# The last stage of a graph network on one core: eight units in the ring of gathered rows in place of six

## The reference, cut to what matters

```python
h = (xn @ W).reshape(N, HEADS, HEAD_DIM)          # 8 heads of 32
a_src = jnp.einsum('nhd,hd->nh', h, att_src)
a_dst = jnp.einsum('nhd,hd->nh', h, att_dst)
e = jax.nn.leaky_relu(a_src[src] + a_dst[dst], NEG_SLOPE)
ee = jnp.exp(e - emax[dst])
alpha = ee / denom[dst]
agg = jax.ops.segment_sum(h[src] * alpha[:, :, None], dst, num_segments=N)
out = layer_norm(agg.reshape(N, 256) + xn @ W_res + bias, ln2_g, ln2_b)
x = x + out + gelu_tanh(out @ ffn_w1 + ffn_b1) @ ffn_w2 + ffn_b2
# then, on the normed x: eight experts of three 256x256 layers each (batch norm, relu),
# summed with softmax weights, and added to x
```

## Time and profile before

| | us |
|---|---|
| median of the timed runs | 2847.34 |
| span of the profiled execution | 3261.7 |
| the last stage in it, from its first gather to its end | 1461.2 to 3261.7 |
| TensorE matmul busy, whole span | 2445.7 (75%) |
| VectorE busy | 1927.4 (59%) |
| GpSimd busy | 1783.5 (55%) |
| ScalarE busy | 1330.1 (41%) |
| gathers of the last stage (line 2766), 784 | 905.8 busy |

### The profile page before, as it was taken

One profiled execution on the slowest core, in us unless ns is written; L12 is line 12 of the kernel. 1 busy time (PEld: TensorE's weight loads), 2 busy tenths in 40 slices (PEclk: granted clock), 3 DMA queues, 4 the chain that ended last, 5 costly groups with the idle time before them and its releaser, 6 DMA issues.

```text
span 3261.7 us, 50094 instructions
## 1 busy us (share of the span) xinstructions
PE 2445.7 (75%) x16869; PEld 1988.4 (61%) x16869; DVE 1927.4 (59%) x5122; ACT 1330.1 (41%) x2771; POOL 1783.5 (55%) x1695
## 2 busy tenths in 40 slices
PE   8437677567676768661567888899888898898998
PEld 8325455345554547660356766777677676686887
DVE  8733344344344447764466676677776676686754
ACT  6303233222222324440234454555544555464665
POOL 6366666666666660837665574465744556464000
PEclk9667777778877778785688998999998999898999
DMA  9443334334443331276467675576765767576534
GB/s 324 142 129 113 118 117 122 110 109 118 119 121 118 113 100 28 88 227 184 138 208 235 191 233 158 181 233 206 224 204 161 219 198 219 177 219 193 160 119 140
DMA packets 312865, 531.11 MB, mean 163 GB/s; under 512 B 89679, under 2 KB 210322, under 8 KB 312598
## 3 DMA queue, kind: packets, MB, share of 16 engines
q1 hardware_dynamic: 234021, 312.19, 30.5%
q0 software_dynamic: 75264, 212.04, 22.8%
q10 hardware_dynamic: 3312, 3.55, 0.4%
HBM read 454.05 MB, written 73.54 MB: 162 GB/s over the span
## 4 chain that ended last, share of the span: by engine, by line
PE 30%; another core or an unknown queue 9%; DVE 6%; issue 5%; ACT 2%; POOL 1%; DMA 1%; SPq 1%; DVEq 0%; POOLq 0%; ACTq 0%
PE PB L125 25%; PE PB L2793 2%; POOL G L2766 1%; DVE G L3092 1%; ACT TFm L3006 1%; DVE XR L3273 1%; DVE H2l L3261 1%; PE PB L2804 0%; DVE H1l L3261 0%; DMA G<-tab,SRCL 0%; PE PB L2845 0%; DVE HT9l L3182 0%; PE PB L2814 0%; PE PB L2880 0%
## 5 line engine op out<-in xcount | busy, mean ns | idle before, releaser
L2766 POOL DMA_INDIRECT G<-tab,SRCL x784 | 905.8, 1155 | 694.8 <-PE PB L2793 442.8
L1194 POOL DMA_INDIRECT GE<-tab,SRCL x748 | 724.0, 968 | 393.9 <-issue 204.1
L3006 ACT ACTIVATE TFm<-PB,BIA,SCL 128x512 f32<-128x512 f32 (+2 forms) x416 | 312.8, 754 | 474.4 <-PE PB L125 226.0
L125 PE MATMUL PB<-YTMh,MW 128*128 128x512 f32 (+2 forms) x832 | 303.8, 416 | 51.6 <-ACT TFm L3006 36.4
L125 PE MATMUL PB<-H1h,MW 128*128 128x512 f32 (+2 forms) x832 | 299.8, 412 | 37.9 <-issue 29.0
L125 PE MATMUL PB<-MW,H2h 128*128 128x256 f32 x1568 | 301.4, 291 | 27.3 <-issue 20.3
L125 PEld LDWEIGHTS PB<-MW,H2h 128*128 128x128 f32 x1568 | 253.9, 197 | 36.1 <-issue 24.9
L3092 DVE TENSOR_TENSOR G<-G 128x1024 f32<-128x1024 f32 x196 | 238.1, 1216 | 2.7 <-DVE G L3086 2.2
L125 PE MATMUL PB<-MW,H2l 128*128 128x256 f32 x784 | 224.7, 287 | 4.7 <-issue 4.7
L1578 ACT ACTIVATE TF<-PB,fb 128x256 f32<-128x256 f32 (+1 forms) x200 | 93.6, 472 | 323.1 <-remote 165.9
L125 PEld LDWEIGHTS PB<-YTMh,MW 128*128 128x128 f32 x832 | 167.7, 204 | 93.9 <-issue 42.8
(11 more groups left out here) (365 smaller groups left out, 6614.6 us busy)
## 6 DMA issues: line engine op xcount, KB each, us to landing
MW<-msplit SPq DMA_DIRECT2D x312, 512.0 KB
ROW<-relrow SPq DMA_DIRECT2D x196, 96.0 KB
msplit<-FWs SPq DMA_DIRECT2D x68, 256.0 KB
part<-ZERO SPq DMA_DIRECT2D x2, 6600.0 KB
G<-tab,SRCL POOLq DMA_INDIRECT x784
GE<-tab,SRCL POOLq DMA_INDIRECT x748
part<-WIN SPq DMA_DIRECT2D x262, 33.0 KB
SUMa<-part SPq DMA_DIRECT2D x49, 132.0 KB
```

The lines of the kernel that those rows point to most:

```text
L125: ins = pe.matmul(ps, lhs(p), rhs(q), start=(first and i == 0), stop=(last and i == 2), skip_group_check=True)
L1194: po.indirect_dma_start(c.GE[:, (s - 2 * UE) % RU, q, 0:256], None, c.tab0, bass.IndirectOffsetOnAxis(ap=c.SRCL[:, 2 * s + q:2 * s + q + 1 ...
L2766: po.indirect_dma_start(b.G[:, j % RP, u, :], None, c.tab1, bass.IndirectOffsetOnAxis(ap=c.SRCL[:, 4 * j + u:4 * j + u + 1].bitcast(U32), ...
L3006: a.activation(b.TM[:, m, 0:n], PB[of][:, 0:n], ACT.Relu, bias=b.BIA[:, l, q:q + 1], scale=b.SCL[:, l, q:q + 1]).then_inc(S.h2_relu if l e ...
```

## The change

The ring of gathered rows gets two more places, and its semaphores two more names. `RP` stands in the allocation of `G8` (`[P, RP, 4, 272]`, 4,352 bytes per partition and place), in GpSimd's wait and place, in VectorE's and TensorE's place, in the count that VectorE waits for (`64 * (j // RP + 1)`) and in the scheduler's rule above.

```diff
-RP = 6
+RP = 8
@@ def g_in(S, r):
-    return (S.g_in0, S.g_in1, S.g_in2, S.g_in3, S.g_in4, S.g_in5)[r]
+    return (S.g_in0, S.g_in1, S.g_in2, S.g_in3, S.g_in4, S.g_in5, S.g_in6, S.g_in7)[r]
@@ def last_layers(nc, c, A, out):
-    S = named(nc, c, "last", "dve consts g_in0 g_in1 g_in2 g_in3 g_in4 g_in5 nd_in0 ...
+    S = named(nc, c, "last", "dve consts g_in0 g_in1 g_in2 g_in3 g_in4 g_in5 g_in6 g_in7 nd_in0 ...
```

More of the change, by code:

```diff
@@ L3291, in last_layers @@
 def last_layers(nc, c, A, out):
-    S = named(nc, c, "last", "dve consts g_in0 g_in1 g_in2 g_in3 g_in4 g_in5 nd_in0 nd_in1 nd_in2 nd_in3 row_in0 row_in1 rowhot onehot "
+    S = named(nc, c, "last", "dve consts g_in0 g_in1 g_in2 g_in3 g_in4 g_in5 g_in6 g_in7 nd_in0 nd_in1 nd_in2 nd_in3 row_in0 row_in1 rowhot onehot "
                              "nd_mm factor product edge_mm evac placed sum_in0 sum_in1 sums self_in0 self_in1 self_in2 self_in3 "
```

## The result

The changed kernel takes 2823.2 us (median of 4 runs, 2819.75 to 2827.59) against 2848.71 us for the kernel before (4 runs, 2845.98 to 2856.44). The ratio is 0.9903, 95% interval 0.9885 to 0.992: 25 to 28 us faster, where 7 us were forecast and 2828 us was the lower end of the range.

What follows compares the result with a forecast made beforehand. TensorE was taken to carry the last stage, with 227 us idle in its middle part. Removing one late-gather event gave 7 us, order counted 0: 2847.3 - 7 = 2840.3 us; 8-in-10 range 2828 to 2859 us.

Steps and rivals of the forecast that it cites:

- the ring runs tight more often than here: Timed runs: if gather instructions don't shrink with the rest, 980 us of gathers stand in a shorter last stage.
- The mechanism: Units 109 to 111: GpSimd's ring wait makes gathers late, VectorE waits at line 3083, TensorE stops 4.45 and 0.99 us.
- The number of places: Last stage from 1580 us: one late-gather event on the chain, units 109 to 111; units 57, 72 and 168 outside it.
- one event of 7.5 us on the chain: Units 109 to 111: VectorE's waits of 0.18, 1.13 and 6.23 us all go; 7 us taken as the gain.
- Rival 3: Ring tight in every 48-unit repeat of the timed runs: 13 to 18 us off, about 2832 us; chance 0.14.
- The limit by VectorE: At units 109 to 111, VectorE without its 6.23 us wait is busy without a break, so at most 7.5 us gained.
- The order: Planner reads RP, so later due times may reorder every engine's list; counted 0, range -11 to +11 us.
- Rival 4: Later due times make VectorE delay weigh and sums; TensorE idle grows 5%: +11 us, 2858 us; chance 0.25.
- The start-up and the last unit: Start-up doesn't count, ring not yet full; unit 195 loses its 34.44 us gather wait but gains nothing in the same order.
- What would show it: Changed trace: line 2793 wait some 400 us, gather waits under 2 us after 1600 us, no late-gather TensorE stop over 4 us.
- The 76.1 us under the name of the first layer's gather: Line 3083 waits from 1580 us on, attributed to some other transfer; 76.1 us should stay after the change.
- earlier gathers would slow others: Gathers brought forward share 16 DMA engines with the weights; part of the "nothing" rival, 2847 us, chance 0.25.

Runs made afterwards that it cites:

- eight with the small memset: Changed kernel plus a 128x128 GpSimd memset ahead of each unit: ratio to the kernel before 0.9991 at 3250 us speed; 2827.45 us, 0.9923 at the other.

## Why the prediction was wrong, point by point

**The trace was that of another speed.** This is the step that failed. The prediction said that the timed runs were not this trace, that the gather instruction would not shrink with the rest, and that "the ring runs tight more often than here", and then took the forecast from the trace all the same. At 2856 us the last stage took 2854.4 - 1307.0 = 1547 us against 1801 us in the earlier trace rows, and GpSimd's gathers needed 1000.07 us of it against 905.85 us. The prediction's own figure for that case, 196 x 5.0 = 980 us, was too small as well: a unit took 1229.9 / 196 = 6.3 us. GpSimd's share of the stage went from 50% to 65%, and in its middle from 55% to 73% (741.93 of 1014 us).

**The mechanism was right.** A ring wait, then gathers that come too late, VectorE at line 3083, a split queued behind it, TensorE stopped and its clock down: the walk through the earlier trace rows holds step for step at units 72 to 74. The price of a place was right in kind too: the longest of the three waits there is followed by two stops of TensorE, 2.38 and 1.05 us, and a clock of 0.56.

**The number of places was mis-sized.** This is the term of the sum that the wrong trace spoiled. The sum had one event of 7.5 us on the chain and 3.2 us of waits outside it, 10.7 us in all behind the start-up. At the right speed line 3083 waited 33 us for gathers behind unit 65, in five places. Rival 3 had this, with the repeat every 48 units and unit 72 and 168 as its evidence, and gave 2832 us with a chance of 0.14; its own price, three or four times 4.45 us, was too small as well. It left out what the forecast counted: the lower clock behind each stop, 12.3 us of TensorE's busy time. Whether 7 us would be right at the 3250 us speed is not shown: that would be a ratio of 0.998, and the interval of seven places there, 0.9971 to 1.0084, takes in both 0.998 and 1.

**The limit by VectorE** ("it can't give more than 7.5 us", the waits of one event) held roughly: at units 72 to 74 the changed kernel gained 7.5 us (from 1.1 us behind at unit 71 to 6.4 us ahead at unit 78) with 6.5 us of waits removed, at 105 to 115 5.4 us with 8.0.

**The order.** Rival 4 and the -11 to +11 us of the range rested on lists that would change, since the due time of the sums came from a gather in 53 of 66 windows. The steps of the last stage came in the same order in both traces. A looser due time changes nothing as long as the same step is still first among those that are ready. This could have been bounded better, and it took 0.25 of the chances.

**The start-up and the last unit** were called worth nothing, and were: the lead below unit 65 gives a ratio of 0.9995. GpSimd's wait before unit 195 (34.44 us in the earlier trace rows, 22.73 us at the other speed) is gone, and from line 3083 of unit 195 to the end it is 206.1 us before (2648.27 to 2854.4) and 206.2 us after (2619.72 to 2825.9).

**What would show it.** Line 3083 was to have under 2 us of waits for gathers behind 1600 us; the changed kernel has 19 us, the last of them at unit 67, and none behind it, where the kernel before has 33 us. No stop of TensorE over 4 us was to stand behind a late gather; one does, 4.42 us behind unit 63. By the first of these signs, taken literally, the mechanism was wrong. Both lie in the tail of the start-up, where GpSimd waited for the ring of six 0.5 us at most; the prediction had let the start-up end at 1580 us, and here it reaches to unit 67. GpSimd's wait for line 2793 was to fall little; it fell from 97.8 to 29.4 us, 22.7 us of it before unit 195, and the last gather ended 63 us earlier (2571.4 against 2634.6 us). The 76.1 us under the name of the first layer's gather are absent from the traces at the faster speed, so what they were is open.

**The Trainium skill** ("DMA: Bandwidth & Descriptors", Rules for kernel authors) tells to issue a DMA early and wait for it late, since its fixed cost, given on that page as about 2.0 us, then overlaps. That is what the change does, and the trace agrees on the direction: 25 us. The figure is short here: where line 3083 waited for a gather in the changed kernel, it started 1.9 to 6.4 us after the end of the last gather instruction, 3.3 us in the median. The section Issuing engines are not separate DMA queues says that DMAs of all engines run on the same 16 DMA engines and interleave; the prediction took from it that earlier gathers would slow others. The DMA engines were 0.80 busy in the middle stage against 0.78, and the stretch still became 28 us shorter.

## What to carry to other kernels

Before a trace is used to size an effect, compare its span with the timed runs; where they differ by a seventh, as here, the waits in it can be those of another balance, and a stream that looks ahead of its reader may be close to the bound. A ring is deep enough when the last gather of the longest burst behind a full ring lands before it is read: here that took one unit of 5 us more, and the second brought nothing. To find where depth counts, vary the lead over stretches of the loop without changing the buffer.

## What the runs showed that I had not expected

One program, unchanged, takes 2850 us on two chips and 3250 us on a third, 14% more. The gather instruction is no slower there (median 947 ns against 951 ns), and ScalarE and VectorE are busy for the same time within 1%. The last stage of the kernel before at 3236 us and at 2856 us, columns as in the earlier trace rows:

```profile
1460.00:3235.00 1775.00, 1453.38 (x10066) 1206.25 (x10066) 1192.68 (x3110) 857.12 (x1505) 919.97 (x784) 0.89 0.64 194
```
```profile
1306.00:2854.00 1548.00, 1369.64 (x10066) 1158.21 (x10066) 1187.66 (x3109) 860.64 (x1505) 1000.11 (x784) 0.94 0.73 222
```

TensorE is busy 84 us longer for the same matmuls, at a clock of 0.89 against 0.94, and idle 322 us against 178 us. Part of that idle time stands where the profile shows nothing: the waits of line 125 in this stage, matmuls and weight loads, at 3236 us and then at 2856 us:

```profile
PE PB L125 <- issue: 77.7, 74, 6.6
PEld PB L125 <- issue: 134.4, 143, 6.7
```
```profile
PE PB L125 <- issue: 1.6, 2, 1.3
PEld PB L125 <- issue: 43.4, 66, 2.8
```

What holds TensorE there is open; no experiment was made on it. It does change what a kernel is bound by: at 3250 us the two deeper rings that were tried (seven places; eight with the small memset) gave nothing within 0.7%. The changed kernel itself was not run at that speed.

A GpSimd memset of 0.23 us between gathers cost 0.09 us of the stream's time, and one of 0.52 us cost 0.39 us: of the 0.3 us that stand before each gather in any case, some 0.14 us hid other work.
